# The last four token tiles of a transformer block: a bank each, products tile by tile, scale and offset on ScalarE

## The reference

```python
x = x + _layernorm(attn(_layernorm(x)))
x = x + _layernorm(ffn(_layernorm(x)))

def ffn(xt):                       # E, TOPK, H, I, NSH = 8, 2, 256, 640, 2
    scores = sigmoid(xt @ w_router.T)
    topk_w, topk_i = top_k(scores, TOPK); topk_w = topk_w / sum(topk_w)
    expert_out = (silu(xt @ wg[e].T) * (xt @ wu[e].T)) @ wd[e].T      # each e
    out = sum(comb[t, e] * expert_out[t, e])
    out = out + sum over the 2 shared experts of (silu(xt @ sg[j].T) * (xt @ su[j].T)) @ sd[j].T
```

## Time and profile before

| | us |
|---|---|
| median of 3 runs | 666.75 |
| lowest and highest run | 665.57, 670.29 |
| span of the profiled execution | 665.1 |
| PE, DVE, ACT, POOL busy in it | 633.5, 531.7, 417.6, 324.8 |

### The profile page before, as it was taken

How to read it: one execution, slowest core, us unless ns; L and a number is a source line. 1 busy time by engine, 2 the same in 40 slices (tenths; PEclk the granted TensorE clock), 3 DMA queues, 4 the chain that set the end, 5 groups by cost and what they waited for, 6 DMA issues and landing times.

```text
span 665.1 us, 15276 instructions
## 1 busy us (share of the span) xinstructions
PE 633.5 (95%) x5914; PEld 514.7 (77%) x5914; DVE 531.7 (80%) x1052; ACT 417.6 (63%) x782; POOL 324.8 (49%) x519
## 2 busy tenths in 40 slices
PE   8987899999999979999989999999999999999994
PEld 6753455555655547888889999999999999888883
DVE  5689999999988743479868888888988888468895
ACT  2426788888887875542257777787877787422230
POOL 3225657767666762100375454545454530178854
PEclk9989999999999999999999999999999999999998
DMA  3853633645550000000376786777776773032221
GB/s 100 165 126 69 113 83 67 129 99 155 103 89 18 19 10 17 17 0 1 119 246 224 239 288 217 260 247 249 249 263 237 248 235 138 24 90 85 88 65 47
DMA packets 79672, 87.10 MB, mean 131 GB/s; under 512 B 54353, under 2 KB 69073, under 8 KB 79601
## 3 DMA queue, kind: packets, MB, share of 16 engines
q0 software_dynamic: 11872, 54.53, 24.9%
q1 hardware_dynamic: 67456, 31.21, 19.5%
q10 hardware_dynamic: 272, 0.39, 0.2%
HBM read 63.83 MB, written 9.31 MB: 110 GB/s over the span
## 4 chain that ended last, share of the span: by engine, by line
PE 75%; DVE 11%; issue 3%; ACT 3%; SPq 2%; DMA 2%; POOL 2%; DVEq 0%; POOLq 0%; another core or an unknown queue 0%; ACTq 0%
PE PS L542 71%; DVE NM L1034 3%; DVE NM L1030 2%; PE PS L553 2%; PE PS L748 1%; DMA X<-in_x 1%; ACT PF L889 1%; SPq L1543 1%; POOL PF L1452 1%; POOL RS L1395 1%; SPq L1549 1%; DMA XG<-xn,XIDX 1%; DVE X L1299 1%; PE PS L697 1%; DVE RR L995 1%
## 5 line engine op out<-in xcount | busy, mean ns | idle before, releaser
L1239 DVE TENSOR_TENSOR HF<-SS,PS 128x256 f32<-128x256 f32 (+2 forms) x141 | 68.6, 487 | 68.4 <-ACT SS L935 29.1
L1318 DVE TENSOR_TENSOR WL<-RAW,WH 128x768 fp32r<-128x768 f32 x125 | 118.4, 958 | 4.4 <-ACT WH L844 3.7
L935 ACT ACTIVATE SS<-PS 128x256 f32<-128x256 f32 (+2 forms) x141 | 62.0, 439 | 81.3 <-PE PS L542 69.6
L1452 POOL TENSOR_SCALAR_AFFINE_SELECT PF<-PF 128x512 f32<-128x512 f32 x128 | 83.5, 677 | 56.0 <-ACT PF L889 55.4
L542 PE MATMUL PS<-WH,HH 128*128 128x256 f32 x355 | 103.2, 291 | 1.2 <-DVE HL L1332 1.0
L844 ACT ACTIVATE HH<-HF 128x256 fp32r<-128x256 f32 (+1 forms) x120 | 58.0, 484 | 72.5 <-DVE HF L1239 61.6
L844 ACT ACTIVATE WH<-RAW 128x768 fp32r<-128x768 f32 x125 | 103.3, 841 | 0.0
L889 ACT ACTIVATE PF<-PS 128x1536 f32<-128x1536 f32 x64 | 92.9, 1452 | 16.5 <-PE PS L542 14.8
L542 PE MATMUL PS<-WL,HH 128*128 128x256 f32 x355 | 100.3, 282 | 0.0
L542 PE MATMUL PS<-WH,HL 128*128 128x256 f32 x355 | 100.2, 282 | 0.0
L542 PE MATMUL PS<-XGL,WH 128*128 128x256 f32 x320 | 90.5, 283 | 0.0
(11 more groups left out here) (203 smaller groups left out, 1468.4 us busy)
## 6 DMA issues: line engine op xcount, KB each, us to landing
ys<-YO SPq DMA_DIRECT2D x16, 256.0 KB
RAW<-in_wsh SPq DMA_DIRECT2D x4, 768.0 KB, 5.0
XT<-in_xt SPq DMA_DIRECT2D x8, 256.0 KB, 3.6
X<-in_x SPq DMA_DIRECT2D x8, 256.0 KB, 3.8
xn<-YY SPq DMA_DIRECT2D x16, 128.0 KB, 1.7
out<-X SPq DMA_DIRECT2D x16, 128.0 KB
ys<-YO SPq DMA_DIRECT2D x7, 128.0 KB
RAW<-in_wsh SPq DMA_DIRECT2D x2, 384.0 KB, 4.8
```

The source lines that it names most:

```text
L935: eng.activation(ss, both(i, bank(b))[0], ACT.Silu).then_inc(free[b] if dense(i) else silu, 1)
L1239: eng.tensor_tensor(hf, ss, both(c, bank(b))[1], ALU.mult).then_inc(free[b], 1)
L1318: eng.tensor_tensor(WL[q % 2][:, c], RAW[raw_of(q)][:, c], WH[q % 2][:, c].bitcast(F32), ALU.subtract).then_inc(w_lo, 1)
L1452: eng.affine_select(out=o, in_=o, pattern=[[0, 4], [1, 128]], base=0, channel_multiplier=-1, compare_op=ALU.is_ge, fill=0.0).then_inc(zero ...
```

## The change

- The last two chunks' `down` become one stage `ends`: down(NC-2) for tiles 12 and 13, down(NC-1) for tiles 12 and 13, then both chunks for tile 14, then both for tile 15. `dn4` is raised after each tile.
- In the last group each tile has a bank of its own (4, 5, 6, 7), over all five chunks.
- `last` on DVE goes tile by tile: wait for the tile, add, BN, MV. The subtractions for tiles 14 and 15 go. For tile 15 DVE also makes VE, and POOL the power only.
- A new stage `scale`, one tile behind `last`: DVE makes -mean * RS in a 128x1 operation (into VE), and ACT computes RS * ACC + that, in place, with Identity.
- `finish` for all four tiles is an add on DVE (X1 + ACC); POOL has no part in it. The list's end is last 12, last 13, scale 12, last 14, scale 13, last 15, scale 14, finish 12, finish 13, scale 15, finish 14, finish 15.
- SP stores tiles 12 to 14; ACT issues the store of tile 15.

```diff
-        if 2 <= c < NC + 2:
+        if c == NC:
+            out.append(("ends", 0))
+        elif 2 <= c < NC:
             out.append(("down", c - 2))
...
             for t in range(4):
                 out.append(("last", LAST4 + t))
-            out.extend(("finish", LAST4 + t) for t in range(4))
+                if t:
+                    out.append(("scale", LAST4 + t - 1))
+            out.extend((("finish", LAST4), ("finish", LAST4 + 1), ("scale", NT - 1), ("finish", LAST4 + 2), ("finish", NT - 1)))
...
-            for b in (4 + sequence(s[1]) % 2,) if DENSE <= s[1] < LAST else (4, 5):
+            for b in (4 + sequence(s[1]) % 2,) if DENSE <= s[1] < LAST else (4, 5, 6, 7) if s[1] == NC - IC else (4, 5):
...
-            def down(c):
+            def down(c, tiles=None):
...
-                for k in range(parts):
-                    b = 4 + k // 2 if dense(c) else 4 + q % 2
-                    lies = 0 if narrow(c) else k % 2
+                for k in range(parts) if tiles is None else tiles:
+                    apart = c >= NC - IC
+                    b = 4 + k if apart else 4 + k // 2 if dense(c) else 4 + q % 2
+                    lies = 0 if narrow(c) or apart else k % 2
...
-                    if c == NC - 1 and k % 2:
+                    if c == NC - 1:
                         t.then_inc(dn4, 1)
-                if c < NC - 1:
+                if c < NC - 1 and k == parts - 1:
                     t.then_inc(dn, 1)
...
+                elif what == "ends":
+                    down(NC - 2, (0, 1))
+                    down(NC - 1, (0, 1))
+                    for t in (2, 3):
+                        down(NC - 2, (t,))
+                        down(NC - 1, (t,))
...
+                elif what == "scale":
+                    e.wait_ge(l_nb, i - LAST4 + 1)
+                    eng.activation(ACC[:, i, :], ACC[:, i, :], ACT.Identity, bias=VE[:, i:i + 1], scale=RS[:, i:i + 1]).then_inc(l_n, 1)
+                elif what == "finish" and i == NT - 1:
+                    e.wait_ge(o_z, 4)
+                    eng.dma_start(out[128 * i:128 * i + 128, :], X1[:, i, :]).then_inc(d_out, 16)
...
-                    b = use["down", NC - IC, 4 + t // 2][0]
-                    if t % 2 == 0:
-                        e.wait_ge(dn4, t // 2 + 1)
-                        for u in range(2):
-                            e.wait_ge(ymix, 2 * (i + u) + 2)
-                            eng.tensor_tensor(ACC[:, i + u, :], bank(b, 256 * u, 256 * u + 256), ACC[:, i + u, :], ALU.add).then_inc(l_acc, 1)
+                    b = use["down", NC - IC, 4 + t][0]
+                    e.wait_ge(dn4, t + 1)
+                    e.wait_ge(ymix, 2 * i + 2)
+                    eng.tensor_tensor(ACC[:, i, :], bank(b, 0, 256), ACC[:, i, :], ALU.add).then_inc(l_acc, 1)
...
-                    if i >= NT - 2:
+                    if i == NT - 1:
                         e.wait_ge(o_mv, i + 1)
-                        eng.tensor_scalar(ACC[:, i, :], ACC[:, i, :], MV[:, i, 0:1], None, ALU.subtract, ALU.bypass).then_inc(l_acc, 1)
+                        eng.tensor_scalar(VE[:, i:i + 1], MV[:, i, 1:2], EPS, None, ALU.add, ALU.bypass).then_inc(l_ve, 1)
+                elif what == "scale":
+                    e.wait_ge(o_rs, i + 1)
+                    eng.tensor_scalar(VE[:, i:i + 1], MV[:, i, 0:1], RS[:, i:i + 1], -1.0, ALU.mult, ALU.mult).then_inc(l_nb, 1)
                 elif what == "finish":
-                    e.wait_ge(o_rs, i + 1)
-                    if i < NT - 2:
+                    if i < LAST4:
+                        e.wait_ge(o_rs, i + 1)
                         normed(ACC[:, i, :], ACC[:, i, :], i).then_inc(o_n, 1)
                     else:
-                        e.wait_ge(l_acc, i - NT + 7)
-                        eng.scalar_tensor_tensor(out=X1[:, i, :], in0=ACC[:, i, :], scalar=RS[:, i:i + 1], in1=X1[:, i, :],
-                                                 op0=ALU.mult, op1=ALU.add).then_inc(o_z, 1)
+                        e.wait_ge(l_n, i - LAST4 + 1)
+                        eng.tensor_tensor(X1[:, i, :], X1[:, i, :], ACC[:, i, :], ALU.add).then_inc(o_z, 1)
...
+                elif what == "last" and i == NT - 1:
+                    e.wait_ge(l_ve, 1)
+                    eng.tensor_tensor(RS[:, i:i + 1], VE[:, i:i + 1], mhalf[:, :], ALU.pow).then_inc(o_rs, 1)
```

More of the change, by code:

```diff
@@ L455, in build @@
         dn4, l_acc, o_z = sem("dn4"), sem("l_acc"), sem("o_z")
+        l_ve, l_nb, l_n = sem("l_ve"), sem("l_nb"), sem("l_n")
         zero, bare = sem("zero"), sem("bare")
@@ L1499, in _ @@
                     deviation(i, o_ve, o_rs, i)
-                elif what == "finish" and i < NT - 2:
+                elif what == "finish" and i < LAST4:
                     e.wait_ge(o_n, i + 1)
@@ L1580, in _ @@
                         shared(1, NK + 1, k)
-                elif what == "finish":
-                    if i < NT - 2:
+                elif what == "finish" and i < NT - 1:
+                    if i < LAST4:
                         e.wait_ge(o_y, i + 1)
                     else:
-                        e.wait_ge(o_z, i - NT + 3)
+                        e.wait_ge(o_z, i - LAST4 + 1)
                     eng.dma_start(out[128 * i:128 * i + 128, :], X1[:, i, :]).then_inc(d_out, 16)
```

## The result

| | before | changed |
|---|---|---|
| median of 21 runs, us | 667.44 | 665.09 |
| lowest and highest | 665.21, 672.55 | 662.80, 668.09 |
| span of the profiled execution, us | 665.1 | 661.7 |

The ratio is 0.9963 with a 95% interval of 0.9948 to 0.9977: 2.4 us less, between 1.5 and 3.5. The forecast was 665.0, no more than 1% from no change, and both hold. That 665.09 falls on 665.0 so closely is partly luck: the forecast took 1.75 off a median of 666.75, while 2.35 came off a median that more runs put at 667.44. One term of its sum does not hold, and it takes the experiments to see which.

A forecast was written before the change was run, and what follows sets the result against it. TensorE, 95% busy, was taken as the bound until the closing tiles, then DVE, POOL and SP's store order; 0.95 from the start plus 0.83 from the ending made 1.78 us less, 665.0 by the median, range 662.9 to 667.3.

The forecast's parts named there:

- First add, 0.95 earlier: Last two chunks' products reordered: DVE's first closing add starts at 653.72 in place of 654.67, 0.95 us won.
- Banks: Banks 6 and 7 for tiles 14 and 15: worth nothing, at most 0.36 us were the cover gone.
- DVE's tile rhythm: DVE's closing tiles: 0.99 us per tile, 0.09 per scale between, 0.1 lost before scale(12), last MV ending at 658.04.
- RS 15 beside DVE's adds: POOL's RS of tile 15 takes 0.91 us beside DVE's finish(12) and finish(13), against 0.58 undisturbed.
- ACT: Scale and offset on ScalarE: 0.606 us per tile; a table load of 1.28, if wanted, hidden by ACT's idle time.
- Last store: Tile 15's store is issued by ACT at 660.62 in place of 662.40, behind none of the other stores.
- the same 2.70: From the last store's issue to the end of the span: 2.70 us as before, so the end at 663.3.
- Sum: Last store's issue 1.78 us earlier: 0.95 from the earlier start, 0.83 from the ending; 1.3 to 2.5 won, chance 0.66.
- Mutual hindrance: Rival: POOL and DVE hinder each other more in the ending; 1.0 us lost, 0.8 won, 666.0; chance 0.14.
- the stores set the end: Rival: the last four stores, not the tiles, set the end; 0 to 0.5 us won, 666.5; chance 0.07.
- The late store from ACT's queue: Rival: tile 15's store from ACT lands 4.6 us after issue; 1.1 us slower, 667.9; chance 0.05.

The follow-up runs named there:

- the first half alone: Kernel before with only the new product order, bank per tile and tile-by-tile adds, old endings and stores: last store at 9.72, end at 12.44 from the start.
- POOL busy late: Changed kernel plus one idle 128x1 memset on POOL behind DVE's last add: span ends at 12.34 in place of 10.88.
- POOL adds tile 13: Kernel with tile 15 ended on DVE, but POOL adds tile 13 after RS 15 and DVE finishes 12, 15, 14: last store at 8.47, end at 11.36.

## Why the prediction was right, and where it was not

- **First add, 0.95 earlier.** Right: 2.43 before, 1.48 after, with the wait for NC-1's HL in its place and about the size forecast.
- **Banks.** Nothing was to be seen, as forecast: the run of matmuls ahead has no new wait, and once the wait for HL is over, a product starts every 0.12 with four banks in use.
- **DVE's tile rhythm.** Right, if a little short: 0.99 forecast and 1.02 found without a scale between two tiles, 1.18 and 1.08 forecast and 1.21 and 1.11 found with one; the 0.1 forecast as lost before scale 12 was there. The last MV ends at 5.91, forecast 5.80; the 128x1 scales took 0.18 to 0.21 where I had 0.165 from a 128x8 row.
- **RS 15 beside DVE's adds.** The direction was right, the size was not: 0.78 for a forecast of 0.91, 0.55 when alone. The Trainium skill (SBUF — State Buffer, "Who interferes with whom") makes the wait last to the end of what started first. Here finish 12 ended 0.38 after RS 15 began, and RS 15 became 0.23 longer. POOL's add of tile 13, in the experiment, ended 0.66 after DVE's operation began, and that became 0.46 longer. So in this case the one that starts second is indeed the one that is held up, but each time by less than a full wait to the end of the other.
- **ACT.** Right: four scalings of 0.60, no table load.
- **Last store.** Forecast 8.38 from the start (660.62 - 652.24), found 8.33. ACT's queue contributed nothing: SP issues the same store at the same time.
- **From the last store to the end, "the same 2.70".** This step was wrong, though its size came out near (2.71 before, 2.55 after), which is luck. The forecast itself put the last landing 1.0 ahead of the end and did not ask what lay between. Before, this stretch was not a store's at all: POOL's DRAIN, 3.37 behind POOL's last add, ended 0.45 after SP was done. The stores could have left 0.86 earlier for nothing, and did so in an experiment. What the change won at the end is that POOL's last computation went from 9.28 to 6.96, as its two adds of 0.9 moved to DVE. After, the two are level: DRAIN done at 10.33, SP at 10.28.
- **Sum.** Forecast 1.78, in the trace 1.99, by the medians 2.35 with 1.5 to 3.5. In the forecast's own terms it was 0.95 from the start, 0.88 from the ending (0.83 forecast) and 0.16 from the last store to the end, where it had nothing. By what bounds the end: the DRAIN would allow 12.64 - 10.33 = 2.31; 0.32 go to a longer way from the last DRAIN to the barrier (0.23 before, 0.55 after).
- **Rivals.** Mutual hindrance is real (0.23) but small. That the stores set the end was wrong for the kernel before and is half true for the changed one. The late store from ACT's queue was wrong; of the Trainium skill's statement (DMA: Bandwidth & Descriptors, "Issuing engines are not separate DMA queues") that a second issuer saves issue time only, this case agrees: 1.74 and 1.70 us to landing, and here no issue time was there to be saved.

What stays open is the 0.32. It is there in every kernel with the new endings, with tile 15's store on ACT or on SP, and in none with the old endings, the first half alone among them. The closing records say where it lies: at POOL's last two semaphore instructions. Here they are in the changed kernel, then in the one with POOL busy late:

```
661.19 661.21 GpSimd EVENT_SEMAPHORE
661.59 661.61 GpSimd EVENT_SEMAPHORE
```

```
661.71 661.73 GpSimd EVENT_SEMAPHORE
661.80 661.82 GpSimd EVENT_SEMAPHORE
```

They start 0.40 apart in the changed kernel, 0.08 apart before: there the delay lies between them. Where POOL has one instruction more (POOL adds tile 13, POOL busy late) they start 0.09 apart, and the first starts 0.36 behind the end of POOL's DRAIN, where it was 0.04: there the delay lies ahead of both. So the delay stays at the same place counted from the start of POOL's instructions, which speaks for the number of instructions ahead of it, or the program's layout, and against the 128x1 operations. No run was made to test that. Nor is it known what POOL's DRAIN does in 3.37 us, only that this does not vary with what ran before it: an add, a power or a memset.

## What to carry to other kernels

Look for what each engine does after its last computation before you tune the last computation: here the end was set by an engine whose last computation had ended 3.4 us before its DRAIN did, and the views of the profile end too soon to show it. Let the engine with the longest closing step finish first; take it out of the last steps even where its work there looks hidden behind a queue of stores. And where two halves of a change feed the same chain, try them apart: the early start gave 0.44 alone and 0.95 with the ending that could use it.

## What the runs showed of the hardware

- POOL's DRAIN at the end of the program ends 3.35 to 3.37 us after POOL's last computation, in fourteen profiles, whatever that computation was (an add of 128x256, a power or a memset of 128x1). SP's takes 0.01. A 0.1 us memset on POOL after the last add of DVE moved the program's end by 1.46.
- The last store, 128 KB, lands 1.70 to 1.74 us after its issue when the one before it left 0.7 us or more earlier, 1.83 when it left 0.5 earlier (the kernel before), and 2.07 when four leave within 1.0 us.
- A POOL add and a DVE operation with two inputs in SBUF hinder each other: DVE's 0.48 became 0.94 behind an add of 0.72, and ended 0.28 after it. A 128x1 power on POOL beside DVE adds with two inputs in SBUF went from 0.55 to 0.78; beside a DVE operation with one it took 0.59.
- The same kernel's last 13 us repeat to 0.02 us between executions, while its whole time varies by several us; almost all of that variation lies ahead of the last products.
